# A two-layer graph network with residual norms on one core: fillers, clears and the load of x moved in the schedule

## The chip, the cores and the metric

The kernel runs on one core of a Trainium2 chip. The metric is the device time of one execution in microseconds (us). The time before is 335.67 us, the median of three runs (334.77 to 335.86).

## The reference, cut to what matters

There are N = 1024 nodes with 512 features and E = 16384 edges, sorted by `dst`. Two graph layers follow each other, each with a residual and a layer norm.

```python
# first layer: dense adjacency from the edges, symmetric normalization, two linear maps, leaky ReLU
A = zeros((1024, 1024)).at[src, dst].add(edge_weight)
deg = sum(A, axis=1); dinv = where(deg > 0, deg ** -0.5, 0)
h = x
for l in range(2):                        # the drawn weights have two steps here
    h = (dinv[:, None] * A * dinv[None, :]) @ h
    h = h @ W_gcn[l] + b_gcn[l]
    h = leaky_relu(h @ W_mlp[l] + b_mlp[l], 0.01)
x = layernorm(x + h)
# second layer: GCN convolution with self loops on the counts of edges
h = relu(gcn_conv(x, src, dst, W1, b1)); h = gcn_conv(h, src, dst, W2, b2)
out = layernorm(x + h)
```

## The kernel before, in words

**Numbers.** Products in full precision are made of three products of halves: each f32 operand is split into a `high` part (rounded by ScalarE, ACT) and a `low` part, the difference (made by VectorE, DVE). `split_product` (L639, its matmuls recorded at L650) does high x high, low x high and high x low. Wg @ Wm is formed ahead of time for each of the two steps (`wc0`, `wc1`, four blocks of 128 rows each), since the two linear maps follow each other directly.

**The loop over edges.** The first part of the kernel builds the adjacency `adj` and the edge counts `cnt`. The edges are cut into CH = 128 chunks of 128. For each chunk TensorE (PE) multiplies a one-hot matrix of sources `sel` with four one-hot or weighted matrices of destinations `hot` (0 is the count, 1 to 3 are the weight in three bf16 terms), so that every chunk is four matmuls of 96 columns at L708. Since the edges are sorted by destination, a chunk touches a window of 12 destinations whose place is read from registers (`load_offsets`, 16 chunks at a time). The windows lie in regions of 52 destinations. Region r sits in PSUM banks 0 and 1 when r is even, 2 and 3 when it is odd. It is opened by `clear(r)` (two matmuls with zeros, L686 or L692) ahead of chunk `opening[r]`, and closed by chunk `closing[r]`. ACT then copies it out (`evacuate`, two copies where r is even, four where it is odd). `clear(r)` waits until region r-2 is copied out. The closing chunks are 8, 14, 21, 27, 34, 40, 47, 53, 60, 66, 73, 79, 86, 92, 99, 105, 112, 118, 125, 127; the openings from region 2 on are 11, 18, 24, 31, 37, 44, 50, 57, 63, 70, 76, 83, 89, 96, 102, 109, 115, 122. Thus two chunks of PE lie between the closing of an even region and the clear that waits for it, and three after an odd one.

**Batches.** DVE makes `sel` and `hot` for ten batches of chunks that begin at chunks 0, 4, 8, 16, 32, 48, 64, 80, 96 and 112. A batch is five instructions (`make(n, 0)` is `sel` at L996, `make(n, 1)` is the count at L999, `make(n, 2)` to `make(n, 4)` are the weight terms at L1004). For the batches in `SHARED` the fifth is not made by DVE but by ACT, chunk by chunk (`scale_columns`, 16 activations that read `last_term`). A batch uses one of three buffers and waits until the batch that had it is used. `make_hw` makes the right side of the degree matmuls (L714); from chunk 34 on these go along with each chunk.

**Fillers.** Between chunks PE does other work, at places written out by hand in `fillers`: `wgt0` and `wgt1` are the transposes of Wg, four blocks each (L636); `wc0` and `wc1` are the products with Wm (12 matmuls a block, which can be cut by k into parts of three matmuls); `bias0`, `biasb0`, `bias1`, `biasb1` are bias products; `prep 4` are two transposes for the test whether the windows cover all edges. Every filler takes a bank of 5, 6, 7 in turn and waits in `claim` for the reader of its last content. After a filler ACT makes the high part and DVE the low part (`lower_fill`). `split_wm` (ACT) and `lower_wm` (DVE) split Wm; `wc0` can't start before `wm_low` and `wgt_low` are whole. `take_flag` on DVE (eight small instructions, L1031 to L1043) reads the result of `prep 4`, which sets `flag_ready`.

**Ends.** Windows that straddle two regions leave ends that DVE adds later (`add_ends(n)`, two instructions, L1070 and L1072). The spare copies of the ends use memory of `adj` five regions ahead, hence this in `evacuate`:

```python
for n, (b0, b1) in enumerate(BOUNDARIES):      # [(1, 4), (5, 8), (9, 12), (13, 14), (15, 16), (17, 19)]
    if b0 + AHEAD == r:                        # AHEAD = 5
        act.wait_ge(head_added, 2 * (n + 1))
```

so that region 6 can't be copied out before `add_ends(0)`, nor region 14 before `add_ends(2)`, and `add_ends(n)` itself waits for the copies of its last region.

**Behind the loop.** After chunk 127 and the last block of `wc1`, the adjacency is transposed and split, x is scaled by `dinv` and split (`upper_x` on ACT waits for `x_in`), and the rest is long rows of split products up to the output. The order of work on each engine is the order of the program text; nothing is planned at run time. All loads are issued by SP in program order; SP waits for `done["biasb1"]` and for all scaled columns before it loads x.

Of the kernel before, what the change touches and what calls it, by code (L numbers as in the profile page):

```python
# [14 lines left out]
P = 128  # L15
# [16 lines left out]
def gnn_resnorm(nc, x, src, dst, weight, wg, bg, wm, bm, w1, b1, w2, b2, out):  # L32
# [29 lines left out]
    assert b0 == CH  # L62
    NBATCH = len(BATCHES)

    SHARED = {4: {21: 6, 27: 10}, 5: {40: 16}, 7: {66: 8, 73: 8}}
    batch_of = {b: n for n, (b, _) in enumerate(BATCHES)}

    with ExitStack() as ctx:
# [145 lines left out]
        def columns(n):  # L214
# [20 lines left out]
        ring = []  # L235


        fillers = {3: [("wgt0", 0, 0, KD)], 10: [("wgt0", 1, 0, KD), ("wgt0", 2, 0, KD)], 15: [("wgt0", 3, 0, KD)],
                   27: [("wc0", 0, 0, KD)], 31: [("wc0", 1, 0, KD), ("prep", 4, 0, KD)], 34: [("wc0", 2, 0, 2)],
                   40: [("wc0", 2, 2, KD), ("wc0", 3, 0, 2)], 47: [("wc0", 3, 2, KD), ("bias0", 0, 0, KD)],  # L240
                   53: [("biasb0", 0, 0, KD), ("wgt1", 0, 0, KD), ("wgt1", 1, 0, KD)],
                   60: [("wgt1", 2, 0, KD), ("wgt1", 3, 0, KD)], 66: [("bias1", 0, 0, KD)],
                   73: [("biasb1", 0, 0, KD), ("wc1", 0, 0, 2)], 79: [("wc1", 0, 2, KD)], 86: [("wc1", 1, 0, 2)],
                   92: [("wc1", 1, 2, KD)], 99: [("wc1", 2, 0, 2)], 105: [("wc1", 2, 2, 3)], 112: [("wc1", 2, 3, KD)],
                   CH - 1: [("wc1", 3, 0, KD)]}
        stops = sorted(set(closing) | set(fillers))
        filling = [(name, i) for c in sorted(fillers) for name, i, k0, k1 in fillers[c] if k1 == KD]


        loads = {15: [16], 31: [32], 47: [48, 64], 73: [80], 86: [96], 105: [112]}  # L250
        ring += [("prep", 0, 5), ("prep", 1, 6), ("prep", 2, 7), ("prep", 3, 4), ("deg", 0, 4)]
        n_fill = [0]

# [94 lines left out]
        @block.sync  # L348
        def _(sp):
            rows, by_k = "(c e) -> c e", "(k p) n -> p k n"  # L350
            sp.dma_start(dst_i[:], dst.rearrange(rows, e=P)).then_inc(dst_in, 16)
            sp.dma_start(src_i[:], src.rearrange(rows, e=P)).then_inc(src_in, 16)
            sp.dma_start(w_e[:], weight.rearrange(rows, e=P)).then_inc(w_in, 16)
            sp.dma_start(wg_raw[:], wg[0].rearrange(by_k, p=P)).then_inc(wg_in, 16)
            sp.dma_start(wm_raw[:], wm[0].rearrange(by_k, p=P)).then_inc(wm_in, 16)
            with nc.allow_non_contiguous_dma(reason="bias columns"):
                sp.dma_start(bg_raw[:], bg[0].rearrange("(k p) -> p k", p=P)).then_inc(bg_in, 16)
                sp.dma_start(b1_t, b1.rearrange("(k p) -> p k", p=P)).then_inc(b1_in, 16)
            sp.dma_start(bias_rows[2:3, :], bm[0:1, :]).then_inc(bm_in, 16)
            sp.wait_ge(done["wgt0"], KD)  # L360
            sp.dma_start(wg_raw[:], wg[1].rearrange(by_k, p=P)).then_inc(wg_in, 16)
            sp.dma_start(wm_next[:], wm[1].rearrange(by_k, p=P)).then_inc(wm_next_in, 16)
            sp.wait_ge(bg_split, 1)
            with nc.allow_non_contiguous_dma(reason="bias columns"):
                sp.dma_start(bg_raw[:], bg[1].rearrange("(k p) -> p k", p=P)).then_inc(bg_in, 16)
            sp.wait_ge(done["biasb0"], 1)
            sp.dma_start(bias_rows[2:3, :], bm[1:2, :]).then_inc(bm_in, 16)
            sp.wait_ge(done["biasb1"], 1)
            sp.wait_ge(scaled, G * len(SHARED))
            sp.dma_start(x_raw[:], x.rearrange(by_k, p=P)).then_inc(x_in, 16)  # L370
            sp.wait_ge(done["h1"], 2 * KD)
            sp.dma_start(xs[:], x.rearrange(by_k, p=P)).then_inc(x_again_in, 16)
            sp.wait_ge(done["h2"], NB)
            sp.dma_start(w1_raw[:], w1.rearrange(by_k, p=P)).then_inc(w1_in, 16)
            sp.dma_start(w2_raw[:], w2.rearrange(by_k, p=P)).then_inc(w2_in, 16)
            sp.wait_ge(taken["h2"], NB)
            sp.dma_start(bias_bc[:], b2.rearrange("(a n) -> a n", a=1).broadcast_to([P, D])).then_inc(b2_in, 16)
            for b in range(NB):
                sp.wait_ge(out_ready, b + 1)
                sp.dma_start(out[b * P:(b + 1) * P, :], xs[:, b, :]).then_inc(stored, 16)  # L380
            sp.wait_ge(stored, 16 * NB)
# [71 lines left out]
        def _(act):  # L453
# [69 lines left out]
            for c in stops:  # L523
                if c in closing:
                    evacuate(closing.index(c))
                for name, i, k0, k1 in fillers.get(c, []):
                    if k1 == KD and name != "prep":
                        upper_fill(name, i)
                for n, parts in SHARED.items():
                    if c in parts:  # L530
                        scale_columns(n, sum(v for k, v in parts.items() if k < c), parts[c])
                if c == 3:
                    split_wm(0, range(3))
                if c == closing[0]:
                    split_wm(0, range(3, KD))
                if c == 47:
                    split_wm(1, range(KD))

            def upper_at(name, h, j):
# [5 lines left out]

            def upper_x(j):
                if j == 0:
                    act.wait_ge(x_in, 16)
                    act.wait_ge(dinv_ready, 1)
                copy(x_high[:, j, :], x_raw[:, j, :], scale=dinv[:, j:j + 1]).then_inc(x_high_made, 1)  # L550

# [61 lines left out]
        def _(pe):  # L613
# [145 lines left out]


            pe.wait_ge(consts, 12)
            pe.wait_ge(off_ready, 1)
            pe.wait_ge(column_ready, 1)
            load_offsets(0)
            LATE_HW = 35
            for c in range(CH):
                if c in batch_of:
                    pe.wait_ge(made, sets_made(batch_of[c]))
                    if batch_of[c] in SHARED:
                        pe.wait_ge(scaled, G * (1 + list(SHARED).index(batch_of[c])))  # L770
                for r in range(NR):
                    if opening[r] == c:
                        clear(r)
                ins = chunk(c)
                if c in closing:
                    ins.then_inc(region_done, 1)
                if c >= LATE_HW:
                    ins = degree(c)
                    if c + 1 in batch_of:
                        ins.then_inc(batch_used, 1)  # L780
                    if c == CH - 1:
                        ins.then_inc(loop_done, 1)
                if c == LATE_HW - 1:
                    pe.wait_ge(hw_made, 1)
                    for k in range(LATE_HW):
                        ins = degree(k)
                        if k + 1 in batch_of:
                            ins.then_inc(batch_used, 1)
                for name, i, k0, k1 in fillers.get(c, []):
                    filler(name, i, k0, k1)  # L790
                for c0 in loads.get(c, []):
                    load_offsets(c0)
                if c == closing[8]:
                    pe.wait_ge(flag_ready, 1)
                    uncovered = pe.value_load(flags[0:1, 0:1], min_val=0, max_val=1)
# [147 lines left out]
        def _(dve):  # L943
# [148 lines left out]
            def make_all(n):  # L1092
                for k in range(5):
                    make(n, k)

            make_all(1)
            make_all(2)
            make(3, 0)
            lower_fill("wgt0", 0)
            for k in range(1, 5):  # L1100
                make(3, k)
            lower_fill("wgt0", 1)
            lower_fill("wgt0", 2)
            lower_wm(0)
            lower_fill("wgt0", 3)
            make_all(4)
            check_windows()
            dve.wait_ge(spill_ready, 1)
            make_hw()
            lower_fill("wc0", 0)  # L1110
            lower_fill("wc0", 1)
            make_all(5)
            take_flag()
            lower_fill("wc0", 2)
            add_ends(0)
            make_all(6)
            lower_fill("wc0", 3)
            make(7, 0)
            lower_wm(1)
            for i in range(2):  # L1120
                lower_fill("wgt1", i)
            for k in range(1, 5):
                make(7, k)
            for i in range(2, KD):
                lower_fill("wgt1", i)
            add_ends(1)
            make_all(8)
            make(9, 0)
            make(9, 1)
            add_ends(2)  # L1130
            for k in range(2, 5):
                make(9, k)
            lower_fill("wc1", 0)
            lower_fill("wc1", 1)
            uncovered = dve.value_load(flags[0:1, 0:1], min_val=0, max_val=1)
            add_ends(3)
# [232 lines left out]
```

## Time and profile before

| what | value |
|---|---|
| median of three runs | 335.67 us |
| the profiled execution, its own time | 335.47 us |
| its span, first to last instruction | 333.6 us |
| PE busy | 314.5 us (94%) |
| DVE busy | 189.0 us (57%) |
| ACT busy | 122.0 us (37%) |

The span is 1.87 us shorter than the execution's own time; the rest lies around the span. PE's busy time includes the tail of the last matmul of a run, so a wait of PE is shown some 0.17 us shorter than what it takes from the next instruction's start.

### The profile page before, as it was taken

The page shows a single profiled execution, that of the slowest core. Times are in us where ns is not written, and L with a number is a line of the kernel's source. Part 1 is how long each engine was busy: PE and PEld are TensorE (multiplying, and loading weights), DVE is VectorE, ACT ScalarE, POOL GpSimd, SP SyncE. Part 2 cuts the span into 40 slices and gives each one's busy share as a digit, 9 for nine tenths or more (in the row PEclk, how much of TensorE's full clock was granted, in tenths as well). Part 3 has the DMA queues.
Part 4 walks back from the last instruction along what each step waited for, and adds up shares of the span by engine and source line. Part 5 has one row for each costly group of instructions (what it writes and reads, how often), then busy time and mean ns, then how long its engine had stood idle before and what let it go on. Part 6 is the DMA issues. An engine that isn't in the chain of part 4 may idle for free.

```text
span 333.6 us, 4919 instructions
## 1 busy us (share of the span) xinstructions
PE 314.5 (94%) x1977; PEld 259.7 (78%) x1977; DVE 189.0 (57%) x333; ACT 122.0 (37%) x253; POOL 49.9 (15%) x54
## 2 busy tenths in 40 slices
PE   2878999998999999999999999999999999999993
PEld 1767786876788888888888888888888888888882
DVE  6998999714544611165643457675953444225664
ACT  3637889546434401134432013233702444220000
POOL 2100000001005970100000011121680000001111
PEclk9999999999999999999999999999999999999998
DMA  6270000700000000000700000006100000000121
GB/s 211 66 254 2 3 2 0 249 6 2 3 0 1 2 0 0 2 0 0 238 15 0 2 0 0 0 4 226 61 2 0 0 0 2 0 4 33 63 84 73
DMA packets 8590, 13.43 MB, mean 40 GB/s; under 512 B 1906, under 2 KB 2290, under 8 KB 8564
## 3 DMA queue, kind: packets, MB, share of 16 engines
q1 hardware_dynamic: 8564, 13.05, 11.6%
q8 instruction: 20, 0.33, 0.4%
q14 instruction: 6, 0.05, 0.0%
HBM read 10.95 MB, written 2.10 MB: 39 GB/s over the span
## 4 chain that ended last, share of the span: by engine, by line
PE 88%; DVE 7%; issue 2%; ACT 1%; DMA 1%; POOLq 0%; POOL 0%; SPq 0%; ACTq 0%
PE psum L650 75%; PE psum L708 6%; PE psum L636 3%; DVE hot L1004 2%; PE psum L755 1%; DVE sel L996 1%; PE psum L830 1%; DVE hot L999 1%; PE psum L692 1%; DVE wm_low L1089 1%; DVE wgt_low L1076 1%; PE psum L714 1%; DMA src_i<-in_src 1%; PE psum L864 1%; ACT hot L455 0%
## 5 line engine op out<-in xcount | busy, mean ns | idle before, releaser
L441 POOL TENSOR_TENSOR small<-small 128x1 f32<-128x1 f32 x16 | 11.9, 742 | 161.6 <-DVE small L1272 161.6
L708 PE MATMUL psum<-hot,sel 128*128 128x96 bf16 x512 | 32.3, 215 | 2.1 <-DVE hot L1004 1.3
L708 PEld LDWEIGHTS psum<-hot,sel 128*128 128x128 bf16 x512 | 28.4, 101 | 7.5 <-issue 6.9
L650 PE MATMUL psum<-at_high,x_high 128*128 128x512 f32 x64 | 25.8, 403 | 0.6 <-DVE x_low L1200 0.6
L1076 DVE SCALAR_TENSOR_TENSOR y_low<-psum,small,y_high 128x512 fp32r<-128x512 f32 x16 | 11.9, 750 | 24.2 <-ACT y_high L455 24.2
L650 PE MATMUL psum<-at_low,x_high 128*128 128x512 f32 x64 | 25.1, 392 | 0.0
L650 PE MATMUL psum<-y_high,at_high 128*128 128x512 f32 x64 | 25.0, 391 | 0.0
L650 PE MATMUL psum<-cnt,x_high 128*128 128x512 f32 x64 | 25.0, 390 | 0.0
L650 PE MATMUL psum<-at_high,x_low 128*128 128x512 f32 x64 | 25.0, 390 | 0.0
L650 PE MATMUL psum<-cnt,x_low 128*128 128x512 f32 x64 | 25.0, 390 | 0.0
L650 PE MATMUL psum<-y_low,at_high 128*128 128x512 f32 x64 | 24.9, 390 | 0.0
L650 PE MATMUL psum<-y_low,cnt 128*128 128x512 f32 x64 | 24.9, 390 | 0.0
L650 PE MATMUL psum<-y_high,at_low 128*128 128x512 f32 x64 | 24.9, 390 | 0.0
L650 PE MATMUL psum<-y_high,cnt 128*128 128x512 f32 x64 | 24.9, 390 | 0.0
L1076 DVE SCALAR_TENSOR_TENSOR g_low<-psum,g_high 128x512 fp32r<-128x512 f32 x16 | 10.2, 682 | 25.8 <-ACT g_high L455 25.8
L455 ACT ACTIVATE g_high<-psum 128x512 fp32r<-128x512 f32 x16 | 8.6, 608 | 33.1 <-PE psum L650 33.1
L586 ACT ACTIVATE xs<-tmp,small 128x512 f32<-128x512 f32 x8 | 6.5, 816 | 38.3 <-DVE small L1284 38.3
L455 ACT ACTIVATE y_high<-psum,small 128x512 fp32r<-128x512 f32 x16 | 10.9, 688 | 25.1 <-PE psum L650 25.0
L1004 DVE TENSOR_TENSOR hot<-hot,tables 128x1536 bf16<-128x1536 bf16 (+2 forms) x27 | 19.7, 776 | 0.3
L1235 DVE TENSOR_TENSOR tmp<-psum,col_scale 128x512 f32<-128x512 f32 x16 | 11.0, 688 | 14.8 <-PE psum L650 14.8
L1076 DVE SCALAR_TENSOR_TENSOR at_low<-psum,at_high 128x512 fp32r<-128x512 f32 x16 | 10.7, 687 | 15.3 <-ACT at_high L455 15.3
L455 ACT ACTIVATE adj<-psum 128x512 f32<-128x512 f32 (+2 forms) x27 | 12.4, 461 | 15.4 <-PE psum L708 15.4
(185 smaller groups left out, 755.3 us busy)
## 6 DMA issues: line engine op xcount, KB each, us to landing
wg_raw<-in_L_gnn_W_gcn SPq DMA_DIRECT2D x2, 1024.0 KB, 5.5
x_raw<-in_x SPq DMA_DIRECT2D x1, 2048.0 KB, 10.3
xs<-in_x SPq DMA_DIRECT2D x1, 2048.0 KB, 9.3
w_raw<-in_L_gnn_W SPq DMA_DIRECT2D x2, 1024.0 KB, 8.1
out<-xs SPq DMA_DIRECT2D x8, 256.0 KB, 2.0
wm_raw<-in_L_gnn_W_mlp SPq DMA_DIRECT2D x1, 1024.0 KB, 8.2
wm_next<-in_L_gnn_W_mlp SPq DMA_DIRECT2D x1, 1024.0 KB, 8.8
bias_bc<-in_L_gnn_b SPq DMA_DIRECT2D x1, 256.0 KB, 8.2
```

The costliest lines, as they stand in the source:

```text
L441: pool.tensor_tensor(r[:, 1:2], r[:, 0:1], power[:, 0:1], ALU.pow).then_inc(rstd_ready, 1)
L455: return act.activation(dest, source, ACT.Copy, **kw)
L586: act.activation(xs[:, i, :], tmp[:, i % 3, :], ACT.Identity, bias=shift[:, i % 2:i % 2 + 1], scale=rstd[:, 2 * (i % 2) + 1:2 * (i % 2) + ...
L636: ins = pe.transpose(dest[:, n * P:(n + 1) * P], b, ident[:])
L650: ins = pe.matmul(dest, s, m, start=first and n == 0, stop=end and n == len(pairs) - 1, skip_group_check=True)
L692: pe.matmul(ends, none[:], zeros[:, 0:2 * COLS].rearrange("p (h a d) -> p h a d", h=NB, a=2), start=True, stop=False, skip_group_check=True)
L708: ins = pe.matmul(sums[1 if k == 0 else 0], stationary, moving, start=False, stop=False, skip_group_check=True)
L714: return pe.matmul(bank("deg")[:, 0:3 * NB].rearrange("p (a h) -> p a h", a=3), sel[buf][:, own, :], hw[:, :, c, :], start=(c == 0), stop= ...
L755: ins = pe.matmul(b[0:2, :], bg_parts[:, k, :], m[:, k, :], start=(k == 0 and n == 0), stop=(k == KD - 1 and n == 1))
L1004: ins = dve.tensor_tensor(sums(k - 1), sums(0), column(k + 1, COLS), ALU.mult)
L1076: dve.scalar_tensor_tensor(out=dest, in0=tile, scalar=scale, in1=high.bitcast(F32), op0=ALU.mult, op1=ALU.subtract).then_inc(low_made[name ...
L1235: dve.tensor_tensor(tmp[:, r % 3, :], bank(name, n), col_scale[:, h * BANK:(h + 1) * BANK], ALU.mult).then_inc(taken[name], 1)
```

## The change

The fillers, the offsets' loads and the order of DVE's work are rearranged. Regions 0 and 1 are cleared ahead of everything else in the loop, then the four transposes of the first Wg are done, and only then are the first offsets loaded and chunk 0 begun. The parts of the first Wg and Wm are lowered by DVE in front of and within batch 2. The two first blocks of `wc0` stand after chunks 7 and 8. The flag is taken ahead of batch 5. Batches 4 and 5 are no longer shared with ACT. The load of x is cut into eight loads of 256 KB, each of which SP starts once the one before has landed; ACT waits for all eight.

```diff
@@ the top and the lists @@
-    SHARED = {4: {21: 6, 27: 10}, 5: {40: 16}, 7: {66: 8, 73: 8}}
+    SHARED = {7: {66: 8, 73: 8}}
...
-        fillers = {3: [("wgt0", 0, 0, KD)], 10: [("wgt0", 1, 0, KD), ("wgt0", 2, 0, KD)], 15: [("wgt0", 3, 0, KD)],
-                   27: [("wc0", 0, 0, KD)], 31: [("wc0", 1, 0, KD), ("prep", 4, 0, KD)], 34: [("wc0", 2, 0, 2)],
-                   40: [("wc0", 2, 2, KD), ("wc0", 3, 0, 2)], 47: [("wc0", 3, 2, KD), ("bias0", 0, 0, KD)],
-                   53: [("biasb0", 0, 0, KD), ("wgt1", 0, 0, KD), ("wgt1", 1, 0, KD)],
-                   60: [("wgt1", 2, 0, KD), ("wgt1", 3, 0, KD)], 66: [("bias1", 0, 0, KD)],
-                   73: [("biasb1", 0, 0, KD), ("wc1", 0, 0, 2)], 79: [("wc1", 0, 2, KD)], 86: [("wc1", 1, 0, 2)],
-                   92: [("wc1", 1, 2, KD)], 99: [("wc1", 2, 0, 2)], 105: [("wc1", 2, 2, 3)], 112: [("wc1", 2, 3, KD)],
+        FIRST = -1
+        fillers = {FIRST: [("wgt0", i, 0, KD) for i in range(KD)],
+                   7: [("wc0", 0, 0, KD)], 8: [("wc0", 1, 0, KD)], 15: [("wc0", 2, 0, 2)], 21: [("wc0", 2, 2, KD)],
+                   27: [("wc0", 3, 0, KD)], 31: [("bias0", 0, 0, KD), ("prep", 4, 0, KD)],
+                   34: [("biasb0", 0, 0, KD), ("wgt1", 0, 0, KD), ("wgt1", 1, 0, KD)],
+                   40: [("wgt1", 2, 0, KD), ("wgt1", 3, 0, KD)], 60: [("wc1", 0, 0, KD)], 63: [("bias1", 0, 0, KD)],
+                   66: [("wc1", 1, 0, 1)], 73: [("biasb1", 0, 0, KD)], 79: [("wc1", 1, 1, 3)], 86: [("wc1", 1, 3, KD)],
+                   92: [("wc1", 2, 0, 1)], 99: [("wc1", 2, 1, 3)], 105: [("wc1", 2, 3, KD)],
                    CH - 1: [("wc1", 3, 0, KD)]}
...
-        loads = {15: [16], 31: [32], 47: [48, 64], 73: [80], 86: [96], 105: [112]}
+        loads = {15: [16], 27: [32], 31: [48], 60: [64], 63: [80], 79: [96], 99: [112]}
@@ SP @@
-            sp.dma_start(x_raw[:], x.rearrange(by_k, p=P)).then_inc(x_in, 16)
+            for j in range(NB):
+                if j:
+                    sp.wait_ge(x_in, 16 * j)
+                sp.dma_start(x_raw[:, j, :], x[j * P:(j + 1) * P, :]).then_inc(x_in, 16)
@@ ACT @@
-                if c == 3:
-                    split_wm(0, range(3))
-                if c == closing[0]:
-                    split_wm(0, range(3, KD))
-                if c == 47:
+                if c == FIRST:
+                    split_wm(0, range(KD))
+                if c == 31:
                     split_wm(1, range(KD))
...
-                    act.wait_ge(x_in, 16)
+                    act.wait_ge(x_in, 16 * NB)
@@ PE @@
             pe.wait_ge(consts, 12)
+            for r in range(2):
+                clear(r)
             pe.wait_ge(off_ready, 1)
             pe.wait_ge(column_ready, 1)
+            for name, i, k0, k1 in fillers[FIRST]:
+                filler(name, i, k0, k1)
             load_offsets(0)
...
-                    if opening[r] == c:
+                    if r >= 2 and opening[r] == c:
                         clear(r)
@@ DVE @@
             make_all(1)
-            make_all(2)
+            lower_fill("wgt0", 0)
+            make(2, 0)
+            lower_fill("wgt0", 1)
+            lower_fill("wgt0", 2)
+            make(2, 1)
+            lower_fill("wgt0", 3)
+            lower_wm(0)
+            for k in range(2, 5):
+                make(2, k)
             make(3, 0)
-            lower_fill("wgt0", 0)
+            lower_fill("wc0", 0)
             for k in range(1, 5):
                 make(3, k)
-            lower_fill("wgt0", 1)
-            lower_fill("wgt0", 2)
-            lower_wm(0)
-            lower_fill("wgt0", 3)
+            lower_fill("wc0", 1)
             make_all(4)
+            lower_fill("wc0", 2)
             check_windows()
             dve.wait_ge(spill_ready, 1)
             make_hw()
-            lower_fill("wc0", 0)
-            lower_fill("wc0", 1)
-            make_all(5)
+            lower_fill("wc0", 3)
             take_flag()
-            lower_fill("wc0", 2)
-            add_ends(0)
-            make_all(6)
-            lower_fill("wc0", 3)
-            make(7, 0)
-            lower_wm(1)
+            make(5, 0)
+            make(5, 1)
             for i in range(2):
                 lower_fill("wgt1", i)
-            for k in range(1, 5):
-                make(7, k)
+            for k in range(2, 5):
+                make(5, k)
+            add_ends(0)
             for i in range(2, KD):
                 lower_fill("wgt1", i)
+            lower_wm(1)
+            make_all(6)
             add_ends(1)
+            make_all(7)
+            lower_fill("wc1", 0)
             make_all(8)
-            make(9, 0)
-            make(9, 1)
             add_ends(2)
-            for k in range(2, 5):
-                make(9, k)
-            lower_fill("wc1", 0)
+            make_all(9)
             lower_fill("wc1", 1)
```

## Rows read from the trace of the kernel before

**Rows 1.** The page: busy us, share of the span, instructions.
```profile
PE 314.5 (94%) x1977; PEld 259.7 (78%) x1977; DVE 189.0 (57%) x333; ACT 122.0 (37%) x253; POOL 49.9 (15%) x54
```

**Rows 2.** Waits of PE up to 85 us: total us, times, longest.
```profile
PE psum L692 <- ACT cnt L455: 2.7, 3, 1.2
PE psum L686 <- DVE hot L1004: 2.4, 1, 2.4
PE psum L708 <- DVE hot L1004: 1.3, 1, 1.3
PE psum L708 <- issue: 0.6, 2, 0.4
```

**Rows 3.** The chain that ended last: start us, us, what.
```profile
27.00 2.79 PE psum L650 x12
...
30.55 0.87 PE psum L714 x35
...
40.36 1.86 PE psum L755 x8
...
43.64 0.98 PE psum L745 x8
44.62 1.02 PE psum L636 x8
45.65 0.20 PE psum L708 x4
```

**Rows 4.** Timeline of DVE: start us, us, line, out<-in, count.
```profile
9.31 0.69 DVE L996 TENSOR_TENSOR sel<-ramp,tables 128x1024 bf16<-128x1024 bf16 x1
...
18.44 2.49 DVE L1089 TENSOR_TENSOR wm_low<-wm_raw,wm_high 128x512 fp32r<-128x512 f32 x4
20.85 0.69 DVE L1076 SCALAR_TENSOR_TENSOR wgt_low<-psum,wgt_high 128x512 fp32r<-128x512 f32 x1
...
53.01 1.22 DVE L996 TENSOR_TENSOR sel<-ramp,tables 128x2048 bf16<-128x2048 bf16 x1
...
55.13 2.69 DVE L1004 TENSOR_TENSOR hot<-hot,tables 128x1536 bf16<-128x1536 bf16 x3
```

**Rows 5.** Timeline of ACT.
```profile
52.46 2.21 ACT L455 ACTIVATE hot<-hot,last_term 128x96 bf16<-128x96 bf16 x8
...
75.47 0.44 ACT L455 ACTIVATE adj<-psum 128x320 f32<-128x320 f32 x1 [0.72 <-PE psum L708]
...
82.38 0.72 ACT L455 ACTIVATE x_high<-x_raw,small 128x512 fp32r<-128x512 f32 x1
```

**Rows 6.** Timeline of PE, the start and the clears.
```profile
10.19 1.03 PE L636 MATMUL psum<-ident,wg_raw 128*128 128x128 f32 x4
11.05 0.33 PE L708 MATMUL psum<-hot,sel 128*128 128x96 bf16 x4
...
20.02 0.34 PE L692 MATMUL psum<-ramp,none 128*128 128x192 bf16 x2 [0.84 <-ACT cnt L455]
...
42.50 0.33 PE L692 MATMUL psum<-ramp,none 128*128 128x192 bf16 x2
...
76.73 0.61 PE L686 MATMUL psum<-ramp,none 128*128 128x512 bf16 x2 [0.65 <-ACT late_ends L455]
```

**Rows 7.** DMA issues: KB each, median us to landing.
```profile
wg_raw<-in_L_gnn_W_gcn SPq DMA_DIRECT2D x2, 1024.0 KB, 5.5
x_raw<-in_x SPq DMA_DIRECT2D x1, 2048.0 KB, 10.3
out<-xs SPq DMA_DIRECT2D x8, 256.0 KB, 2.0
src_i<-in_src SPq DMA_DIRECT2D x1, 64.0 KB, 1.9
```

**Rows 8.** Windows near the end; the last columns are PEclk, DMA share, GB/s.
```profile
328.00:329.00 1.00, 0.07 (x1) 0.00 (x0) 0.85 (x2) 0.00 (x0) 0.00 (x0) 1.00 0.55 209
...
332.00:333.60 1.60, 0.00 (x0) 0.00 (x0) 0.00 (x0) 0.00 (x0) 0.00 (x0) 0.50 0.44 164
```

## The prediction

> **What bounds the kernel now.** I read the page first: PE is busy 94% of the span, DVE 57%, ACT 37% [rows 1]. So only PE's idle time can be won, and before asking what a moved filler costs on another engine the reader must ask where PE idles. The waits of PE come next [rows 2]: up to 85 us it waits 2.4 us for the first `hot`, 1.3 us for a later one, 2.7 us in three places for a region's copies, 0.7 us once more for such copies at L686 [rows 6], and 0.6 us for nothing shown ("issue"). The chain [rows 3] says that from about 27 us PE's own work follows upon itself, so behind that point each us of a filler is a us of the span wherever it stands. In front of it DVE sets the pace: its timeline [rows 4] has no gap from batch to batch. The change moves no work out of the program on PE; it can win only by moving work under PE's waits, and lose by laying waits bare.
>
> **Unit costs.** A block of `wc` (12 matmuls) takes 2.8 us, half a block 1.47, a quarter 0.79 (the quarter as 2.8/4 plus a tail of 0.09, an estimate); `bias0` 1.87; `biasb0` 0.98; eight transposes 1.02; the 35 degree matmuls 0.87; a chunk with its degree matmul 0.208 (0.20 and 0.01 in the chain), without it 0.18 [rows 3]; a clear 0.17 (half of the 0.34 shown for two matmuls is the tail that the next one overlaps) [rows 6]. On DVE, start to start: a full batch 4.72 (53.01 to 57.73, the last row less its tail of 0.09), of which `sel` and count 2.12, each term 0.87; lowering 0.60 a block (`wm_low`: 18.44 to 20.85 is 2.41 for four) [rows 4]. On ACT, eight scaled columns are 2.15 [rows 5]. The price of a closed region is read from clears that wait [rows 6]: an even one 0.84 idle plus 0.17 tail plus two chunks of 0.18, 1.35 from the end of its closing chunk to its clear; an odd one 0.65 + 0.17 + three chunks of 0.208, 1.44. Between closing and clear only 0.42 or 0.62 of chunks stand, so a closing with no filler behind it costs PE 0.9 (even) or 0.8 (odd).
>
> **Step 1, the start.** The four clears now run behind PE's first transposes, at about 5.6 to 7.3. Wg lands 5.5 us after its issue at 2.1 [rows 7], at 7.6. Its four transposes (0.86 a block, as the one at 10.19 before chunk 4 at 11.05 [rows 6]) run to 11.1; chunks 0 to 7 and their offsets to 13.0. Then `wc0` block 0 waits for `wm_low`. DVE begins batch 2 at 9.31 [rows 4]; ahead of the end of `wm_low` it now has eight blocks to lower (4.8) and two instructions of batch 2 (0.60 and 0.48): 15.3. Thus PE idles 13.0 to 15.5. It has done by then everything that it had done before at about 16, without the old waits at L686 and L708, but a new 2.5 us wait is what paid for that. Batch 2 is whole at 16.9, behind the filler that covers it.
>
> **Step 2, PE without a gap to `prep 4`.** From 15.5: `wc0` four blocks in five parts (11.4), chunks 8 to 31 (24 x 0.18, with four clears 5.0), `bias0` 1.87, `prep` 0.22, some tails: 33.9. The copies of regions 0 to 3 all lie behind a filler each, and DVE is ahead: batch 3 at 23.3, batch 4 (now full, 0.87 more) at 28.6, `make_hw` at 32.6. The old waits at 20.0 and 26.5 are gone.
>
> **Step 3, the flag.** DVE is free for `take_flag` at 33.2 and waits to 34.1 for `prep 4`, then 1.63 to 35.8. Batch 5: `sel` and count to 37.9, `wgt1` 0 and 1 (ACT has the first at 38.1, behind the split of the second Wm and region 4) to 39.35, three terms to 42.0. PE arrives at chunk 48 at 41.4: waits 0.7. **The new wait of this change stands here**: region 6 closes at chunk 47 but can't be copied before `add_ends(0)`, now behind batch 5: 42.0 + 0.93, then ACT: clear 8 runs at 44.2, PE idle 1.6. Before, clear 8 ran at 42.50 [rows 6]. But by then `biasb0` (0.98) and all of `wgt1` (2.04) are done, which before came later. Net: 3.0 - 1.7 = 1.3 us ahead.
>
> **Step 4, the rest of the loop.** From clear 8 to the end of chunk 118 PE has 69 chunks (14.35), eleven clears (1.9), `wc1` 0, 1, 2 in seven parts (9.0), `bias1` 1.87, `biasb1` 1.05: 28.2. Idle: closings 53 (0.8) and 112 (0.9) have no filler any more; `biasb1` takes the bank of `wc1` 0, lowered only behind batch 7 at 56.65 (0.6); scaling batch 7 on ACT stands in front of region 10's copies (0.2), its second half holds up chunk 80 (0.2) and region 11 (0.55); region 12 has 0.1. Sum 3.35, so 44.2 + 31.5 = 75.75, where before it was 75.3 (the wait of 0.65 at 76.73 for region 17 is in both). The old `issue` gaps, 0.6 [rows 2], are not in this sum: one stood behind a quarter filler with a load of offsets, and loads now stand behind longer fillers; the other, while x came in, has no cover that I can name. I put 0.1 to 0.2 of them back. **Net: 0.45 + 0.15, about +0.6 us.** Batch 8 is whole at 61.4 for chunk 96 at 67, batch 9 at 70 for chunk 112 at 73, although DVE waits 3 us in `add_ends(2)` for region 12's copies (64.6), and batch 9 stands behind that; if the 3 us of margin went, this is what would be late next. Behind the loop nothing changes: `wc1` 3 is last in both.
>
> Unsharing two batches costs DVE 1.7 us and gives ACT 32 scaled columns, 8.6 us; DVE has the room except through step 3, where 0.87 of it is hidden in the wait for `prep 4`.
>
> **Step 5, x.** x now starts when the last column is scaled, 61.1. A 256 KB transfer out took 2.0; 64 KB in took 1.9 and 2048 KB in 10.3 [rows 7], a line through these gives 2.7. With 0.1 to wake SP, eight take 16.8 to 22.4: 78 to 83.5. x is needed at 82.4 [rows 5], plus the shift. I take 2.4 a piece, nearer to the transfer of its own size: 81.1, in time by 1.3 us.
>
> The Trainium skill's page "DMA: Bandwidth & Descriptors", section "Anatomy of one DMA", gives each DMA about 2.0 us that doesn't shrink with size, plus bytes by 436 GB/s. The 1.9 for 64 KB agrees. By that rule a piece is an estimated 2.6 us, the eight end at 82.7, and x is late by a few tenths.
>
> **The sum.** The profiled execution is 335.47, the median 335.67. From the former +0.6 is 336.1; the median's side gives 336.3. I predict 336.2 us. Below 0.3% (1.0 us) this measurement can't tell from no change.
>
> **Rivals.** (a) *As summed*, chance 0.48: 335.2 to 337.0. Its own error is the 0.1 to 0.2 us in each of ten waits.
> (b) *The front's lead is kept, faster.* Step 4's waits for ACT's scaling and for `biasb1` (1.55) don't arise, since PE comes to them a bit later than I put it. For it: each is under 0.6 and a PE later by as much swallows it. Against: region copies without filler stay at 1.7 whatever comes. 336.2 - 1.55 = 334.6; chance 0.22.
> (c) *The clock falls in the new wait, slower.* Place: PE's 2.5 us idle at 13.0 to 15.5. Price: `wc0` block 0 at half rate, 2.8 us more, or half of it, and all is passed on, as PE has no gap up to `prep 4`: 337.6 to 339. In the trace the granted clock went to 1.2 GHz (0.50) at the end, where PE's last matmul ended at 328.07 and the records show the lower level from before 332 on [rows 8]: some 3.9 us of idle went ahead. Waits up to 1.3 us inside the loop left it at 2.4 GHz. The new wait is between the two. Chance 0.15. The Trainium skill's page "TensorE: Matmul & The Clock Gate", Part 4, says that transposes don't count as busy for the gate; here 16 of them stand ahead of this wait, which speaks for (c). No row of this trace separates that.
> (d) *x is late, slower.* Place: ACT's `upper_x(0)`. For it: the line's 2.7. It decides above 2.6 us a piece; at 2.7, 1.1 us late: 337.3. Against: the piece out took 2.0. Chance 0.15.
>
> **Numbers.** Faster by more than 0.3%: 0.2 (b, less its near half, and the low edge of a). Within: 0.44 (most of a). Slower: 0.36 (c, d, and the upper edge of a, which is near the bound). Range for 8 in 10: 334.4 to 337.9; a alone 335.2 to 337.0.
>
> **What would show it.** PE idle 13 to 15.5 ending on `wm_low` L1089; wgt transposes by 11; `prep 4` near 33.9; clear 8 at 44.2, released by a copy that came behind `add_ends`; idle behind chunks 53, 112; chunk 118 at 75.7. The line of x: eight issues from 61 on, 2.1 to 2.8 apart, and whether ACT's first `x_high` waits for a DMA. Wrong would be: matmuls of `wc0` block 0 at about twice 0.23 us apart (c); a wait for x (d); or clear 8 well ahead of 44, which would mean that the flag or `add_ends(0)` isn't what holds it.

## The result and the profile after

The changed kernel takes 339.92 us (median of four runs, 339.63 to 340.26), the kernel before 335.22 in the same session; the ratio is 1.014, with an interval of 1.0115 to 1.0165. It is slower by 4.7 us, where +0.6 (336.2) was forecast. The profiled execution has a span of 338.3 us, 4.7 more than before.

The waits of PE up to 95 us, for comparison with [rows 2] (us in total, times, longest); the first wait for the edges (4.5 us here, 4.1 before) and three of 0.6 us and less are left out:

```profile
PE psum L695 <- ACT cnt L460: 2.9, 3, 1.5
PE psum L653 <- DVE wcb_low L1083: 2.8, 1, 2.8
PE psum L653 <- issue: 1.8, 1, 1.8
PE psum L711 <- issue: 1.2, 1, 1.2
PE psum L689 <- ACT late_ends L460: 0.7, 1, 0.7
PE psum L711 <- DVE hot L1011: 0.6, 1, 0.6
```

The waits of 2.4 and 1.3 us for `hot` are gone, as meant. In their place stand two "issue" waits at the start (time in which PE waited for nothing that the profile shows) and one wait that was not there before: 2.8 us for `wcb_low`, the low part of a `wc1` block. The timeline of PE says where they stand:

```profile
12.38 1.66 PE L711 MATMUL psum<-hot,sel 128*128 128x96 bf16 x32 [1.24 <-issue]
15.80 0.47 PE L653 MATMUL psum<-wm_high,wgt_high 128*128 128x512 f32 x1 [1.76 <-issue]
...
44.55 0.34 PE L695 MATMUL psum<-ramp,none 128*128 128x192 bf16 x2 [1.46 <-ACT cnt L460]
...
47.00 0.34 PE L695 MATMUL psum<-ramp,none 128*128 128x192 bf16 x2 [0.65 <-ACT cnt L460]
...
53.97 0.33 PE L711 MATMUL psum<-hot,sel 128*128 128x96 bf16 x4
54.14 0.18 PE L717 MATMUL psum<-hw,sel 128*128 128x24 bf16 x1
57.10 0.50 PE L653 MATMUL psum<-wm_high,wgt_high 128*128 128x512 f32 x1 [2.79 <-DVE wcb_low L1083]
...
58.08 0.54 PE L711 MATMUL psum<-hot,sel 128*128 128x96 bf16 x4
...
58.48 0.54 PE L711 MATMUL psum<-hot,sel 128*128 128x96 bf16 x4
...
62.23 0.34 PE L711 MATMUL psum<-hot,sel 128*128 128x96 bf16 x4
```

The reader is to see three things. Up to clear 8 at 44.55 PE runs near the time of the prediction (44.2). Chunk 66 ends at some 54.3, and then the filler behind it, the first part of `wc1` block 1, waits. And behind that wait the chunks start 0.40 us apart (58.08, 58.48) instead of 0.21. The windows tell why (each row: the stretch, its length, then the busy us of PE, PEld, DVE, ACT and POOL, and at the end the granted clock PEclk, DMA share and GB/s):

```profile
54.50:57.00 2.50, 0.00 (x0) 0.00 (x0) 2.47 (x5) 2.50 (x10) 0.00 (x0) 1.00 0.00 0
57.50:58.00 0.50, 0.50 (x3) 0.13 (x1) 0.50 (x1) 0.14 (x1) 0.00 (x0) 0.69 0.00 0
58.00:61.00 3.00, 3.00 (x37) 2.91 (x37) 2.97 (x5) 0.00 (x0) 0.00 (x0) 0.50 0.00 0
61.00:62.00 1.00, 1.00 (x6) 0.38 (x3) 0.78 (x1) 0.73 (x2) 0.00 (x0) 0.95 0.00 0
62.00:64.00 2.00, 2.00 (x34) 1.74 (x34) 0.00 (x0) 2.00 (x7) 0.00 (x0) 1.00 0.00 0
```

PE did nothing from 54.3 to 57.1. Its granted clock was 0.50, which is 1.2 GHz, from about 57.7 (0.69 is the mean of the half us around that) to about 61.1 (0.95 in the us behind 61), and then 2.4 GHz again.

The timeline of DVE shows what it did while PE waited:

```profile
52.51 1.22 DVE L1003 TENSOR_TENSOR sel<-ramp,tables 128x2048 bf16<-128x2048 bf16 x1
53.64 0.95 DVE L1006 TENSOR_TENSOR hot<-ramp,tables 128x1536 bf16<-128x1536 bf16 x1
54.62 1.83 DVE L1011 TENSOR_TENSOR hot<-hot,tables 128x1536 bf16<-128x1536 bf16 x2
56.37 0.68 DVE L1083 SCALAR_TENSOR_TENSOR wcb_low<-psum,wcb_high 128x512 fp32r<-128x512 f32 x1
```

These are batch 7 (chunks 80 and on; PE reaches chunk 80 at 65.29) and then the low part of `wc1` block 0. Only that last instruction frees the bank. The banks go round in the order in which fillers are *finished*. `wc1` block 1 is begun behind chunk 66 but finished behind chunk 86, so in that order it stands behind `biasb1` (73), and its bank is that of `wc1` block 0, not that of `wgt1`.

x, at last, was loaded in eight pieces of 2.6 us (median from issue to landing):

```profile
x_raw<-in_x SPq DMA_DIRECT2D x8, 256.0 KB, 2.6
```

and the issues on SP take 18.99 us from 65.14 on; ACT's first `x_high` starts at 86.91 right behind its `at_high`:

```profile
65.14 18.99 SPq L375 DMA_DIRECT2D x_raw<-in_x  x8
```

The last piece is issued at 83.8 and lands at about 86.4, half a us before the first piece is used.

### The profile page after: what moved, and what is told of

Its sections match the earlier page's. It is cut to its first block, busy times and chain, and to the rows that moved or that the text cites. A ratio compares the mean times of both kernels' runs of the same rounds, so it can differ in the third digit from the quotient of the medians.

```text
span 338.3 us, 4892 instructions
## 1 busy us (share of the span) xinstructions
PE 316.6 (94%) x1977; PEld 261.0 (77%) x1977; DVE 190.5 (56%) x335; ACT 114.5 (34%) x221; POOL 49.0 (14%) x54
## 4 chain that ended last, share of the span: by engine, by line
PE 84%; DVE 8%; ACT 3%; issue 3%; DMA 1%; POOLq 0%; POOL 0%; SPq 0%
PE psum L653 74%; PE psum L711 5%; DVE hot L1011 3%; PE psum L639 2%; PE psum L837 1%; DVE wgt_low L1083 1%; DVE sel L1003 1%; PE psum L695 1%; ACT cnt L460 1%; DVE wm_low L1096 1%; DMA src_i<-in_src 1%; DVE hot L1006 1%; ACT adj L460 1%; ACT hot L460 1%; ACT wm_high L460 1%
## 5 line engine op out<-in xcount | busy, mean ns | idle before, releaser
L1011 DVE TENSOR_TENSOR hot<-hot,tables 128x1536 bf16<-128x1536 bf16 (+2 forms) x29 | 21.4, 787 | 0.3
```

What stands on the lines that cost most here:

```text
L1011: ins = dve.tensor_tensor(sums(k - 1), sums(0), column(k + 1, COLS), ALU.mult)
```

## The experiments

Three theories stood open. Theory 1: the bank of `wc1` block 0 makes PE wait 2.8 us, and the clock falls behind that wait. Theory 2: the closings that have no filler any more ("bare closings"), and `add_ends(0)`, cost what is lost. A third: the load of x in pieces has a share. e1 to e4 ran together, then e5 to e7, e8 and e9, and e10 in three further sessions; each ratio is to the kernel before in the same session.

**e1: `wc1` block 0 lowered ahead of batch 7**

```diff
             add_ends(1)
+            lower_fill("wc1", 0)
             make_all(7)
-            lower_fill("wc1", 0)
```

> The changed kernel with one move on DVE: the low part of wc1 block 0 ahead of batch 7 instead of behind it. Theory 1 (a bank): the filler behind chunk 66 claims the bank that wc1 block 0 has, which DVE frees only behind batch 7; PE idles 2.8 us for it and then runs 4 us at half clock. It expects 335.7 to 336.6 us, 3.4 to 4.2 below the changed kernel, no wait on wcb_low there and a granted clock of 1.00 from 50 to 70 us. Theory 2 (the bare closings and add_ends(0) are what costs): at most 1 us less, 338.9 or more.

Measured: 336.22 us, ratio 1.0043 (1.0026 to 1.006). One line of DVE moved forward by 3.6 us leaves 1.3 us over the kernel before (334.93 here), where the changed kernel had 4.7 over it (335.22 in its session): 3.4 us come back. The granted clock is 1.00 from 50 to 70 us, and PE from 54 to 57 is busy throughout:

```profile
54.00:57.00 3.00, 3.00 (x55) 2.63 (x52) 2.96 (x4) 2.96 (x11) 0.00 (x0) 1.00 0.00 0
```

Theory 1 holds, and theory 2 can explain no more than the 1.3 us that are left.

**e2: PE kept busy in the wait**

```diff
                 for name, i, k0, k1 in fillers.get(c, []):
+                    if c == 66:
+                        spare = claim("biasb1")
+                        for _ in range(12):
+                            pe.matmul(spare, none[:], ramp4[:].rearrange("p q c -> p (q c)"), start=True, stop=True)
                     filler(name, i, k0, k1)
```

> The changed kernel with twelve matmuls of zeros (512 columns, into the spare bank that biasb1 uses later) in front of the filler behind chunk 66, so that PE is busy while it waits for the bank. If the fallen clock costs on its own: the wait for the bank ends at the same time, the seven chunks behind it run at 0.21 instead of 0.40 us, and the time is 338.3 to 338.9, 1 to 1.6 below the changed kernel. If the fallen clock is hidden by waits for ACT: no change, 339.6 to 340.2.

Measured: 338.32 us, ratio 1.0108 (1.0091 to 1.0125). The wait for the bank ends as before, but PE did twelve useless matmuls meanwhile, and the chunks behind it start 0.21 us apart:

```profile
54.13 2.75 PE L800 MATMUL psum<-ramp,none 128*128 128x512 bf16 x12
57.05 0.50 PE L653 MATMUL psum<-wm_high,wgt_high 128*128 128x512 f32 x1 [0.17 <-DVE wcb_low L1087]
...
57.86 0.34 PE L711 MATMUL psum<-hot,sel 128*128 128x96 bf16 x4
...
58.07 0.36 PE L711 MATMUL psum<-hot,sel 128*128 128x96 bf16 x4
...
60.64 0.34 PE L711 MATMUL psum<-hot,sel 128*128 128x96 bf16 x4
```

```profile
58.00:61.00 3.00, 3.00 (x49) 2.19 (x47) 2.97 (x5) 1.32 (x3) 0.00 (x0) 1.00 0.00 0
```

So the loss splits. The fallen clock is read best from the traces: from the end of the wait to the chunk behind `biasb1` PE takes 57.10 to 62.23, 5.13 us, in the changed kernel and 57.05 to 60.64, 3.59 us, here, so it costs 1.5 us. The medians give 1.6 (339.92 - 338.32), or 1.3 where each is taken over the kernel before in its own session (4.70 and 3.39). Then 338.32 - 336.22 = 2.1 us is the wait itself, and 1.3 us (336.22 against 334.93) is the rest. The wait is 2.79 us idle and 0.17 of tail, more than 2.1, because without it waits for ACT's scaling come to light that it had covered: clears 11 and 13 are 6.08 us apart here and 6.74 in e1.

**e3: the changed kernel with x in one transfer**

```diff
-            for j in range(NB):
-                if j:
-                    sp.wait_ge(x_in, 16 * j)
-                sp.dma_start(x_raw[:, j, :], x[j * P:(j + 1) * P, :]).then_inc(x_in, 16)
+            sp.dma_start(x_raw[:], x.rearrange(by_k, p=P)).then_inc(x_in, 16)
```

> The changed kernel with x loaded by one transfer as before. Theory 1 expects no change (within 0.3 us), x landing near 75.5 us instead of 86.4. A rival that the load of x in pieces costs part of the 4.3 us expects at least 0.5 us less.

Measured: 340.19 us, ratio 1.0151 (1.0104 to 1.0197), which overlaps that of the changed kernel: the pieces have no part in the loss that could be seen. The four runs lie far apart, 337.96 to 341.17, wider than the 0.3 us that was expected, so the medians alone could hide a us or so. The trace says more: x landed at 73.9, and ACT's first `x_high` still came at 86.7 (86.9 with the pieces), so nothing had waited for x. It also shows the clock falling a second time, earlier: from about 44.0 to 47.5 it was 0.50, in and behind the wait of 1.46 at clear 8. PE then came later to the bank, whose wait was 1.95 instead of 2.79.

**e4: the kernel before with x in pieces**: the opposite edit on the old kernel, with ACT waiting for all eight.

> The kernel before with x loaded tile by tile and nothing else. At 2.66 us a piece x lands near 79.6, ahead of its first use at 82.4: no change, 335.0 to 335.7; the 0.39 us gap in a chunk at 66.75 us, if it came from the one big transfer, is gone. The rival that pieces are late expects 336 or more with ACT waiting for x.

Measured: 334.83 us, ratio 0.9996 (0.9986 to 1.0005): no difference. Its pieces took 2.6 us (median; 2.4 to 4.5), from 58.2 on, and ACT didn't wait. The gap of 0.39 us in the middle of chunk 99, which stood at 66.75 while the one big transfer ran, does not appear in this profile, nor does the other `issue` gap of [rows 2]; clears 15 and 16 are 2.95 us apart where they were 3.51 in the profile of before. The medians of the two differ by 0.1 us only.

**e5: e1 with `add_ends(0)` earlier**

```diff
+            add_ends(0)
             for k in range(2, 5):
                 make(5, k)
-            add_ends(0)
```

> The version with the low part of wc1 block 0 ahead of batch 7, and add_ends(0) ahead of batch 5's three terms instead of behind them. The reading that region 6's copies wait for add_ends(0): the 1.46 us idle at clear 8 shrinks to about 0.8 while batch 5 comes 0.93 later; net 0.3 to 0.7 below e1 (336.22), 335.5 to 335.9. The rival that other waits take it up: as e1.

Measured: 336.75 us, ratio 1.0038 (1.0023 to 1.0053), no different from e1. The forecast of 0.3 to 0.7 did come true at its place: chunk 48 now waits 1.57 for batch 5 where it waited 0.64, clear 8 no longer waits 1.46, and clear 8 runs at 43.89 instead of 44.78 (0.2 of that is an earlier start). It was lost behind it. Clear 12 waits 0.89 for ACT's copies where it waited 0.34, and in this profile the clock then fell, from about 59.4 to 62.8:

```profile
43.46 0.34 PE L711 MATMUL psum<-hot,sel 128*128 128x96 bf16 x4 [1.57 <-DVE hot L1011]
...
43.89 0.33 PE L695 MATMUL psum<-ramp,none 128*128 128x192 bf16 x2
...
58.54 0.34 PE L695 MATMUL psum<-ramp,none 128*128 128x192 bf16 x2 [0.89 <-ACT cnt L460]
```

```profile
59.50:62.00 2.50, 2.50 (x12) 2.08 (x11) 2.29 (x3) 2.50 (x10) 0.00 (x0) 0.50 0.00 0
```

Of its six runs three (336.80 to 336.96) have a mean granted clock of 0.991, as the profiled one; the others are 335.76, 335.96 and 336.70. So the rival "other waits take it up" holds in part, and the clock has a share.

**e6: the front of the changed kernel, and a filler behind every closing from 53 to 112**

```diff
-                   34: [("biasb0", 0, 0, KD), ("wgt1", 0, 0, KD), ("wgt1", 1, 0, KD)],
-                   40: [("wgt1", 2, 0, KD), ("wgt1", 3, 0, KD)], 60: [("wc1", 0, 0, KD)], 63: [("bias1", 0, 0, KD)],
-                   66: [("wc1", 1, 0, 1)], 73: [("biasb1", 0, 0, KD)], 79: [("wc1", 1, 1, 3)], 86: [("wc1", 1, 3, KD)],
-                   92: [("wc1", 2, 0, 1)], 99: [("wc1", 2, 1, 3)], 105: [("wc1", 2, 3, KD)],
+                   34: [("wgt1", 0, 0, KD), ("wgt1", 1, 0, KD)],
+                   40: [("wgt1", 2, 0, KD), ("wgt1", 3, 0, KD)], 53: [("biasb0", 0, 0, KD)], 60: [("bias1", 0, 0, KD)],
+                   66: [("wc1", 0, 0, 2)], 73: [("biasb1", 0, 0, KD)], 79: [("wc1", 0, 2, KD)], 86: [("wc1", 1, 0, 2)],
+                   92: [("wc1", 1, 2, KD)], 99: [("wc1", 2, 0, 2)], 105: [("wc1", 2, 2, 3)], 112: [("wc1", 2, 3, KD)],
```

together with e5's move, `wc1` block 0 lowered behind batch 9, the offsets of chunk 80 loaded behind chunk 66, and x in one transfer.

> The front of the changed kernel (up to chunk 40) with a back in which each closing from 53 to 112 has its filler again (biasb0 behind 53, bias1 behind 60, wc1 in two-k and one-k parts from 66 on), add_ends(0) ahead of batch 5's terms, wc1 block 0 lowered behind batch 9 (nothing then waits for its bank before the last block), and x in one transfer. If the front's lead is real and only the bare closings and the bank lose it: 333.3 to 334.6, about 1 us faster than the kernel before. If DVE or ACT takes it up: 335 or more.

Measured: 337.19 us, ratio 1.0063 (1.005 to 1.0076): 0.7 us slower than e1 by ratio (the intervals overlap), and the expectation failed. PE now reaches batch 5 with nothing to do, and behind that its clock fell (from about 45.5 to 48.9):

```profile
43.30 0.34 PE L708 MATMUL psum<-hot,sel 128*128 128x96 bf16 x4 [1.71 <-DVE hot L1008]
```

```profile
44.00:48.00 4.00, 4.00 (x54) 3.92 (x51) 4.00 (x7) 1.35 (x5) 0.00 (x0) 0.69 0.02 5
```

DVE is busy 4.00 of those 4 us. Work of PE moved out of this stretch doesn't shorten it: DVE sets its end, as e7 shows, where PE at full clock waits for batch 6 too.

**e7: e6 with x in pieces**

> The same as e6 with x tile by tile. Measured 2.3 to 2.66 us a piece from a start near 60.5: landing at 79 to 81.8, while x is wanted at about 81. Near the edge: 0 to 1 us slower than e6. If pieces cost nothing: the same as e6.

Measured: 336.3 us, ratio 1.0038 (1.0025 to 1.0051). It is not slower than e6 but 0.9 us faster, which neither branch of the expectation had. In this profile the clock stood at 1.00 from 44 to 48 where it was 0.69 in e6's, and PE waits 1.17 us for batch 6 instead. But the clock doesn't explain the medians: three of e6's runs have a mean clock of 0.997 and are its slowest (337.36 to 337.73), while e7's at 0.995 to 0.998 took 336.20 to 336.38. The way x is loaded is the only other difference. As with the kernel before and e4, clears 15 and 16 are further apart while one big transfer of x runs (3.41 us in e6, 2.94 in e7), but in that first pair the medians hardly differ. The cause stays open.

**e8: e1 with batch 7 not shared**

```diff
-    SHARED = {7: {66: 8, 73: 8}}
+    SHARED = {}
...
-            sp.wait_ge(scaled, G * len(SHARED))
```

> The version with the low part of wc1 block 0 ahead of batch 7, and batch 7 no longer shared with ACT (no scaled columns at all). In e1 the two lots of eight columns (2.15 us each) stand in front of region 10's and 11's copies: waits of about 0.3 at clear 12, 0.25 ahead of chunk 80 and 0.2 at clear 13, while DVE idles 2.9 us in add_ends(2) and can take 0.87 more. If that is the remaining loss: 335.1 to 335.7, 0.5 to 1.1 below e1. If DVE takes it up: as e1 or more, 336.2.

Measured: 335.06 us, ratio 0.9998 (0.999 to 1.0007): level with the kernel before. The 16 scaled columns on ACT, in front of the copies of regions 10 and 11, were most of what was left. Their waits at clears 12 and 13 and ahead of chunk 80 are gone: clears 11 and 13 are 5.70 us apart, 1.04 less than in e1. DVE, which idled 2.91 us in `add_ends(2)` in e1, idles 0.99 there and took the extra term without loss.

**e9: e8 with a filler behind closing 112 again**: the two-k part behind chunk 99 is cut into `99: [("wc1", 2, 1, 2)], 105: [("wc1", 2, 2, 3)], 112: [("wc1", 2, 3, KD)]`.

> e8 with the part of two k behind chunk 99 cut into two of one k, so that closing 112 has a filler again (the wait of 0.75 us at clear 18 goes; closing 99 may wait 0.1 to 0.2). 0.5 to 0.7 below e8: 334.5 to 335.1, level with the kernel before or a little under it. If the wait only moves to region 14 or 15: as e8.

Measured: 335.00 us, ratio 0.9998 (0.9987 to 1.001). The wait of 0.75 at clear 18 is gone in the profile, but the median is 0.06 us below e8 and not 0.5. The twelve runs lie between 334.45 and 336.32, and they part by mean granted clock: the five at 0.990 to 0.993 have a median of 335.63, the seven at 0.995 to 0.999 one of 334.60. Where in the kernel the slower five lost their clock isn't shown, as the profiled run is one of the seven.

**e10: e9 with matmuls of zeros in the waits that are left**

```diff
+            def keep_busy(name, count):
+                spare = claim(name)
+                for _ in range(count):
+                    pe.matmul(spare, none[:], ramp4[:].rearrange("p q c -> p (q c)"), start=True, stop=True)
...
+                if c in (48, 50, 57):
+                    keep_busy("wc1", {48: 2, 50: 7, 57: 3}[c])
...
+                if c == 7:
+                    keep_busy("wc0", 7)
```

> e9 with matmuls of zeros in PE's waits that are left (seven in front of wc0 block 0, two ahead of batch 5, seven ahead of clear 8, three ahead of clear 9; 0.22 us each, less than each wait). The runs of e9 lie from 334.45 to 336.32, and the slow ones among them have a lower mean granted clock (0.990 to 0.993 against 0.999). If the clock's fall in these waits makes the spread: all runs within 334.4 to 334.9, mean clock 0.998 or more, and the median about 0.4 under the kernel before. If the zeros delay PE: 335.0 or more.

Measured: 334.63 us, ratio 0.9989 (0.9978 to 1.0). No run is below 0.995 in clock (the expectation had 0.998), and ten of twelve lie between 334.20 and 334.89; one took 336.21 at a clock of 0.999, which the clock doesn't explain. It is the fastest version here, by 0.1% against the kernel before, which is at the edge of what the interval can tell from nothing, and its interval overlaps that of e9: what the zeros change is the spread rather than a median that is clearly lower. In the waits of PE what had been 1.76, 0.64, 1.46 and 0.65 is 0.2 or gone:

```profile
PE psum L653 <- issue: 0.2, 1, 0.2
PE psum L711 <- DVE hot L1020: 0.2, 1, 0.2
```

## Why the prediction was wrong

The step that failed is in step 4: "`biasb1` takes the bank of `wc1` 0, lowered only behind batch 7 at 56.65 (0.6)". The date was right (in the trace the lowering begins at 56.37) and so was its cause, but the wrong filler was put in front of it. `wc1` block 1 has that bank, begun at 54.2 behind chunk 66, and not `biasb1` behind chunk 73, which comes 2 us later. I had dealt out the banks by the place where a filler begins; the code deals them by the place where it ends. 0.6 should have been 2.8 idle plus the tail of 0.17, so 2.4 us were missing.

The second part of the miss follows from the first. Rival (c), the fall of the clock, was right as a mechanism and wrong in its place. In the wait at the start, 1.76 us of idle after 1.24, the clock did not fall; it fell behind the wait of 2.8 us that I hadn't seen. e2 prices it at 1.5 us by the traces (1.3 to 1.6 by the medians), the lower end of the 1.4 to 2.8 named there. The 2.4 and the 1.5 together are 3.9 of the 4.1 us between the forecast of +0.6 and the measured +4.7. The Trainium skill's page "TensorE: Matmul & The Clock Gate", Part 4, says that transposes don't count as busy in the same way as other matmuls, which I let speak for a fall at the start; here the chunks right behind 16 transposes and the 1.24 us of idle started 0.2 us apart (32 matmuls in 1.66) at a granted clock of 1.00, so nothing of it was to be seen.

Point by point:
- *Step 1.* `wc0` started at 15.80, predicted 15.5. Two waits of 1.24 and 1.76 stand where one of 2.5 was expected: the load of the first offsets, which follows the transposes, costs 1.24 of PE's time instead of being hidden. (That it is this load is argued: the profile names no cause, and the program has nothing else there.) It is absorbed by the wait for `wm_low` behind it.
- *Step 2.* PE had no gap from 15.8 to the end of `prep 4` (34.3, predicted 33.9). Right.
- *Step 3.* The flag was done at 36.2 (35.8), DVE waited 0.82 for it; chunk 48 waited 0.64 (0.7), clear 8 ran at 44.55 (44.2) after 1.46 idle (1.6), behind `add_ends(0)`. Right. e5 showed that moving `add_ends(0)` brings clear 8 forward but not the end.
- *Step 4, the rest.* Closing 53 cost 0.65 as shown, closing 112 0.75, which are the prediction's 0.8 and 0.9 once the tail of 0.17 is added. The scaling on ACT, 0.95 in sum, is confirmed by e8: 1.04 less between clears 11 and 13, and 1.2 us less in all than e1 (336.22 to 335.06, in different sessions; by ratio 0.0045, or 1.5 us). But the sum has an error beside the bank. Its +0.6 holds the 0.6 for the bank, so without that wait the changed kernel should have been level with the kernel before, and e1 stands 1.3 us over it. In e1's profile 0.6 of this is there by clear 8 (44.78 instead of 44.2, of which the later start of `wc0`, 16.02 instead of 15.5, is 0.5), and 0.5 comes behind it (32.9 us from there to clear 19, where the sum less the bank has 32.4). Which terms make up the last 0.5 isn't shown.
- *Step 5.* A piece of x took 2.6 us, not 2.4. The estimate of 2.6 from the page "DMA: Bandwidth & Descriptors" of the Trainium skill came out for this size. But the page gives that fit for transfers issued by GpSimd, and these are issued by SP. For larger ones the traces don't agree: by the same fit 1024 KB would be an estimated 4.4 us and 2048 KB 6.8, where [rows 7] have 5.5 and 10.3. x was still in time, since its use was late by the other 4 us. In e7, with the use near the time of the prediction (83.4), the last piece was issued at 79.3 and landed before it, so that it was no loss either.

Rival (b) can't be judged on the changed kernel, as the front's lead was eaten by the wait. On e1 it can: the waits for ACT's scaling, which (b) took to vanish, arose (the 1.04 us that e8 took away).

What stays open: why one run of e10 takes 1.5 us longer at full clock; why e6 and e7 differ; and when the clock falls in waits like these, which differs from run to run. e9's runs part by their clock. e3's don't: two of them have the same mean clock of 0.993 and took 337.96 and 340.64.

## What to carry to other kernels

When buffers are dealt out by a list, work out that list for the new order before costing any wait: moving the first part of a job ahead of another doesn't move its buffer, and the one number that decides is when the last reader frees it. Put the instruction that frees a shared buffer ahead of long work that is needed only later; here it was one line of 0.6 us that stood behind 3.9 us of work. And a wait of the matmul engine can cost more than its length: the 2.8 us here cost 1.5 more through the clock, so the longest wait is the first that is worth splitting or filling. Short waits close together aren't safe either, as e3, e5 and e6 show.

## What the runs showed of the hardware

In the changed kernel the granted clock fell to 0.50 about 0.6 us behind the end of a wait of 2.8 us, with PE busy again, and stayed there from 57.7 to 61.1. It also fell, in some runs only, where no wait nearby was over 1.8 us: in e3 (waits of 0.65 and 1.46), in e5 (waits of 0.89 and less, 59.4 to 62.8), and in e6, where the mean over the window from 44 to 48 is 0.69, behind 4 us in which PE was busy 2.29. The first line is e3's, the second e6's:

```profile
44.00:48.00 4.00, 3.53 (x44) 3.37 (x45) 4.00 (x7) 1.49 (x5) 0.00 (x0) 0.57 0.00 0
```

```profile
40.00:44.00 4.00, 2.29 (x52) 2.18 (x49) 4.00 (x7) 2.35 (x6) 0.00 (x0) 1.00 0.00 0
```

e7's profile has the same 2.29 us of work in that window and no fall, and the changed kernel's own profile has the waits of e3 at 42.5 and 44.5 and no fall there. With useless matmuls in the wait the clock stayed at 1.00 in e2's profile from 54 to 64, and none of e10's twelve runs has a mean clock below 0.995, where five of e9's are at 0.990 to 0.993.
